# Two head loops written out: ACT and DVE without a loop, POOL with one

## What is computed

```
xn = layernorm(x)
x  = x + L0_attn(xn) + L0_ffn(xn)      # gated delta rule, 32 value heads on 16 key heads; MoE of 64 experts
xn = layernorm(x)
x  = x + L1_attn(xn) + L1_ffn(xn)      # 32 heads of 8, and 8 experts

L0_attn: mixed = conv4(silu)(xn @ w_qkv); q, k, v per head; l2norm(q), l2norm(k)
         for t: S = S*exp(g_t); d = (v_t - k_t S)*b_t; S = S + k_t d^T; o_t = q_t S
         out = (rmsnorm(o * silu(z)) * norm_w) @ w_out
```

## Time and profile before

| | us |
|---|---|
| median of three runs (lowest, highest) | 3089.01 (3083.01, 3095.82) |
| the profiled execution, its own time | 3097.86 |
| its span | 3096.1 |
| PE busy, of the span | 2761.4 (89%) |
| DVE busy | 2385.2 (77%) |
| ACT busy | 1765.9 (57%) |
| POOL busy | 1236.7 (40%) |
| mean granted TensorE clock | 0.963 of 2.4 GHz |

### The profile page before, as it was taken

One profiled execution on the slowest core, in us unless ns is written; L12 is line 12 of the kernel. 1 busy time (PEld: TensorE's weight loads), 2 busy tenths in 40 slices (PEclk: granted clock), 3 DMA queues, 4 the chain that ended last, 5 costly groups with the idle time before them and its releaser, 6 DMA issues. The chain is left out here.

```text
span 3096.1 us, 129193 instructions
## 1 busy us (share of the span) xinstructions
PE 2761.4 (89%) x52495; PEld 2287.1 (74%) x52496; DVE 2385.2 (77%) x5142; ACT 1765.9 (57%) x5625; POOL 1236.7 (40%) x1120
## 2 busy tenths in 40 slices
PE   2599989898999999999999999999999999967888
PEld 1477777777787878787878787878788888744555
DVE  7577787777877777777887878777778787638996
ACT  1366666666666666666666666666666666521111
POOL 4555555655333333333333333333333333335620
PEclk8799999999999999999999999999999999988999
DMA  4211111101111111111110111111111111163311
GB/s 170 73 52 55 42 41 31 31 27 29 44 30 42 30 44 30 44 30 44 30 44 30 44 30 37 29 37 34 39 34 41 34 41 34 34 228 98 115 63 41
DMA packets 94202, 155.58 MB, mean 50 GB/s; under 512 B 17238, under 2 KB 61829, under 8 KB 92403
## 3 DMA queue, kind: packets, MB, share of 16 engines
q1 hardware_dynamic: 69779, 112.45, 12.2%
q0 software_dynamic: 12288, 24.19, 2.5%
q10 hardware_dynamic: 11520, 10.49, 1.0%
HBM read 115.18 MB, written 41.29 MB: 51 GB/s over the span
## 5 line engine op out<-in xcount | busy, mean ns | idle before, releaser
L1278 DVE SCALAR_TENSOR_TENSOR p_y<-p_xr,p_cw,p_y 128x512 f32<-128x512 f32 x768 | 673.4, 885 | 44.3 <-ACT p_y L1027 23.8
L1085 ACT ACTIVATE p_Xs<-p_psI 128x256 f32<-128x256 f32 (+1 forms) x386 | 160.3, 415 | 523.0 <-PE p_psI L762 451.0
L714 PE MATMUL p_psF<-xnS,p_w_hl 128*128 128x512 f32 x1536 | 433.4, 419 | 21.1 <-PEq L586 21.1
L1504 POOL TENSOR_TENSOR p_E<-p_E,p_sj 128x512 f32<-128x512 f32 x128 | 131.8, 1050 | 744.2 <-DVE p_sj L1305 744.2
L714 PEld LDWEIGHTS p_psF<-xnS,p_w_hl 128*128 128x128 f32 x1536 | 278.0, 195 | 74.6 <-issue 21.7
L1323 DVE TENSOR_TENSOR p_ATP<-p_psF,p_E 128x512 f32<-128x512 f32 x256 | 166.5, 687 | 180.6 <-PE p_psF L749 171.6
L1512 POOL TENSOR_TENSOR p_M<-p_ATc,p_masks 128x512 f32<-128x512 f32 x128 | 170.4, 1336 | 308.4 <-ACT p_ATc L1065 308.4
L771 PE MATMUL p_psI<-p_Xs,p_DTc 32*32 32x32 f32 x16384 | 213.6, 196 | 66.6 <-issue 64.6
L762 PEld LDWEIGHTS p_psI<-p_Dc,p_M 32*32 32x32 f32 x16384 | 174.4, 107 | 130.9 <-issue 122.8
L771 PEld LDWEIGHTS p_psI<-p_Xs,p_DTc 32*32 32x32 f32 x16384 | 177.0, 107 | 121.0 <-issue 106.1
L762 PE MATMUL p_psI<-p_Dc,p_M 32*32 32x32 f32 x16384 | 205.5, 195 | 60.0 <-DVE p_DTc L1341 35.2
(11 more groups left out here) (328 smaller groups left out, 6541.1 us busy)
## 6 DMA issues: line engine op xcount, KB each, us to landing
p_ab<-decays SPq DMA_DIRECT2D x64, 512.0 KB, 5.3
p_w_raw<-in_w_in SPq DMA_DIRECT2D x17, 768.0 KB
expert_out<-p_ye ACTq DMA_DIRECT2D x80, 128.0 KB, 2.2
p_wgu<-in_w_gu SPq DMA_DIRECT2D x56, 176.0 KB
expert_in<-p_zero SPq DMA_DIRECT2D x16, 512.0 KB, 9.7
p_xe<-expert_in SPq DMA_DIRECT2D x56, 128.0 KB
p_wd<-in_w_down SPq DMA_DIRECT2D x56, 88.0 KB
p_wout<-in_w_out SPq DMA_DIRECT2D x16, 256.0 KB
```

The lines of the kernel that those rows point to most:

```text
L714: m = pe.matmul(b4(psF[f % 2][:, :]), w_hl[:, wp, kt, ty * P:(ty + 1) * P], xnS[:, xp, kt, :].rearrange("p (b t) -> p b t", b=B)[:, :, c * ...
L1085: act.activation(dst, src, ACT.Copy).then_inc(s["xs" if l < 5 else "join_xs"], 1)
L1278: m = dve.scalar_tensor_tensor(y[:, ty, :, :], xr[:, ty, :, tap:tap + P], cw[:, ty, tap:tap + 1], y[:, ty, :, :], ALU.mult, ALU.add)
```

## The change

ACT's and DVE's loops over the heads become Python loops like PE's. The calls of `announce` and the branch go, and every wait's value becomes a constant. `count[0]` is set to 0 for each head, as the emitted step did it once before. POOL keeps `heads_loop`. Below the first edit line numbers of ACT fall by 2 only after its loop, those of DVE's functions by 2, those of POOL and of layer 1 by 3.

```
-            with heads_loop(nc, "heads_act", mybir.EngineType.Activation, HK) as (kh, announce):
+            for kh in range(HK):
                 for c in range(NC):
-                    if c == NC - 1:
-                        announce()
                     step(kh, c)
...
-            with heads_loop(nc, "heads_dve", mybir.EngineType.DVE, HK) as (kh, announce):
+            for kh in range(HK):
+                count[0] = 0
                 for c in range(NC):
-                    if c == NC - 1:
-                        announce()
                     step(kh, c)
                 assert count[0] == DSTEPS, count[0]
```

## The result

The changed kernel takes 3072.3 us (median of 8 runs, 3066.4 to 3075.9) against 3088.3 for the kernel before (8 runs, 3083.0 to 3099.4): ratio 0.994, 95% interval 0.9926 to 0.9954, so 14 to 23 us faster, 16.0 by the medians. The prediction had 3075. The profiled execution took 3070.1 us, 2.2 under its median, where the one before was 9.6 over its own; so traces that differ by 27.8 us of span stand for 16.0 us, and only what repeats from head to head is read from them. Of the 27.8 us, 13.1 are PE's busy time with the same instructions, at a mean granted clock of 0.963 before and 0.969 after, and 14.7 are PE's idle time. The 16.0 us owe little to the clock: the changed kernel's eight runs have a mean of 0.968, and 23 runs of the kernel before, beside the first experiments, 0.967.

The account below looks back on a forecast made before the run. PE, busy for 89% of the span, bounds the kernel. Late register operations (9.2 us) and the passage between heads (4.4) sum to 13.6 us, taken from the median 3089.0 to predict 3075 us, range 3050 to 3092.

Parts of the forecast that it names:

- Register operations behind a late wait: Where an engine idles for a late semaphore, each register operation delays the data operation 0.08 us; together 9.2 us.
- Covered ones: Register operations beside running data operations, such as the 1712 at DVE's L1269, are worth 0.
- L1341: PE's 64 waits for DVE's transposes in the levels: half counted, 32 x 0.08 = 2.6 us.
- L1323: PE's 16 waits for DVE: two register operations behind PE's first product, 16 x 0.16 = 2.6 us.
- L1333: PE's 16 waits: ACT's copy in front has two register operations behind DVE's products, 16 x 0.16 = 2.6 us.
- keys from ACT: PE's 18 waits for keys: one register operation each, at ACT's evacuation or the silu, 18 x 0.08 = 1.4 us.
- The passage: Between heads: 0.17 us from DVE's earlier taps and 0.12 from ACT's kq, 0.29 x 15 = 4.4 us.
- The table load does not bound the passage: Between heads: DVE's taps bound, so ACT's 1.28 us load adds nothing; PE's wait moves from L897 to L739.
- The range of the forecast: Whole kernel: by the bounds of the prices, the forecast's own range is 3064 to 3084 us.
- rival A: Passage between heads: PE keeps the whole 1.1 us in each head, 16.5 us; time 3059; chance 0.28.
- B: PE's 79 stops before L771 set the pace; the gain shrinks to 0 to 5 us, 3087; chance 0.16.
- C: ACT's and DVE's written-out heads: fetching straight code stalls PE's path, 37 us less 13.6, time 3112; chance 0.11.

Follow-up runs that it names:

- run 10: Changed kernel with one register operation put back before the subtraction of each inverse level (255 places); ratio 0.9966 to the kernel before.
- run 6: Changed kernel with one covered register operation put back into the wait of every link of DVE's chains; ratio 0.992 to the kernel before.
- run 2: Kernel before with only DVE's heads written out, ACT keeping its loop and table loads; ratio 0.9967 to the kernel before, 10.2 us faster.
- run 7: Changed kernel with five register operations in a row before the subtraction of each inverse level; ratio 1.0175 to the kernel before.
- Run 1: Kernel before with only ACT's heads written out, DVE keeping its loop; ratio 0.9985 to the kernel before, 4.6 us faster.
- run 9: Changed kernel with 12 small copies before the Silu opening each head's ACT work, a delay without a load; ratio 0.9961 to the kernel before.
- half changes: Kernel before with only ACT's heads written out (ratio 0.9985), and with only DVE's written out (0.9967).
- runs 1 to 3: Kernel before with ACT's heads alone written out (0.9985), DVE's alone (0.9967); changed kernel with POOL's loop written out too (0.9942); ratios to the kernel before.
- run 8: Changed kernel with POOL's third L537 operation waiting for the next head's key taps, in POOL's loop only; ratio 0.9896 to the kernel before.
- runs 9 to 12: Changed kernel with 12 copies (0.9961); one late register operation a level (0.9966); POOL's third operation later, its loop written out (0.993); later, loop kept (0.9915).

## Why the prediction was right

The time was right to 3 us and the mechanism largely. That the sum came so near is in part luck: two terms were too large by 5.0 us together, and two too small by about 7. Its terms:

- **Register operations behind a late wait, 0.08 us each: right.** 0.087 us between 0.133 and 0.046 behind PE, in over 100 places; put back alone in run 10, the 0.13 returns. **Covered ones 0: right**, run 6.
- **L1341, 2.6 us: too small.** PE's wait fell by 4.1 (4.8 with DVE alone), and run 2 leaves some 7 us for it beside its passages. The step that failed is the count, 32 places: in run 7 half of the delay of all levels in which DVE waits for PE shows in PE's waits, and of such levels the kernel before has 124, so 62 x 0.087 = 5.4 us (an estimate).
- **L1323, 2.6 us: wrong, 0.** PE's wait before L739 for the products stayed at 5.0. In the kernel before and in the changed one, the product that PE waits for starts right behind PE's matmuls:

```profile
209.81 1.13 PE L749 MATMUL p_psF<-p_kq 128*128 128x256 f32 x4
210.97 1.29 DVE L1323 TENSOR_TENSOR p_ATP<-p_psF,p_E 128x512 f32<-128x512 f32 x2 [0.76 <-PE p_psF L749]
```

```profile
208.13 1.13 PE L749 MATMUL p_psF<-p_kq 128*128 128x256 f32 x4
209.30 1.29 DVE L1321 TENSOR_TENSOR p_ATP<-p_psF,p_E 128x512 f32<-128x512 f32 x2 [0.84 <-PE p_psF L749]
```

  0.03 and 0.04 us: this product, the step's second half, never had a register operation behind its late wait. The first half had (0.13 to 0.21 us behind PE before, 0.04 now, in most steps), and PE doesn't wait for that one. The prediction counted from the program's text, where the timeline would have told.
- **L1333, 2.6 us: wrong, 0.2** (5.2 to 5.0).
- **keys from ACT, 1.4 us: about right.** PE stands before L739 also in every step c = 1: 13.0 us in the trace before, 11.8 after.
- **The passage, 4.4 us: too small, 7.4.** The arms were right: no wait before L897, one of 0.85 before L739, which grew by 6.0 us (5 to 12 foretold); the first tap at 0.75; a later one at 1.64 (1.8 foretold). Two sizes were off. POOL holds a tap for 0.9 us and not 1.06, and with the tap's start at 2.97 that makes 0.34 us where 0.17 was expected. ACT's two register operations before kq made 0.155, not 0.12 (kq starts 0.19 behind the third tap before, 0.03 after).
- **"The table load does not bound the passage": true of the kernel before, not of the change.** Run 1 shows it free with DVE in its loop. In run 2, with DVE written out, ACT's loop costs 0.29 us of each passage (7.29 against 7.00), and it is the arm with the load that ends last there (L781 at 7.36; kq, with its register operations, is done at 7.00). A delay of 1.11 us in that place without a load or a loop costs 0.18 (run 9). The prediction counted both edits at once and so got the right sign; a load priced at 0 and left in would cost some 3 to 4 us (15 x 0.18 to 0.29, an estimate).

- **The range of the forecast, 3064 to 3084:** its lower end is no sum of the prices. By their dear ends, 13.8 and 16.5 us, it would be 3059, which stands under rival A.

Terms: 7.4 for the passage and 1.2 for the keys, from the traces, and about 7 for the levels, what run 2 leaves, make 15.6 of 16.0. The last is a remainder and known to 4 us only, so that the sum closes this well is chance.

Of the rivals, **A** (PE keeps the 1.1 us) is refuted by the wait for kq. **B** (the stops before L771 set the pace) would have had them above 75 us: they are 60.0, and 65.8 and 59.5 in the half changes. **C** (fetch of straight code) needed ACT or DVE idle with "issue" for 0.5 us and more off the passages, and a slower kernel; none of runs 1 to 3, in which up to three more engines are written out, is slower than its counterpart, and the queue moves fewer packets. One row has the sign that the prediction named: "ACT L1024 <- issue", 10.6 us in 10 pieces, nine of them over 0.5 us, not there before. Its longest, in the timeline of the changed kernel:

```profile
958.38 4.40 PE L714 MATMUL p_psF<-xnS,p_w_hl 128*128 128x512 f32 x12
...
961.39 0.60 ACT L1024 ACTIVATE p_xr<-p_psF 128x512 f32<-128x512 f32 x1 [2.96 <-issue]
```

PE was in the projection whose first half ACT evacuates there. In all ten pieces ACT starts 0.09 us behind the end of the sixth of its 12 matmuls; where the rows name PE, it starts 0.04 us behind the end of that same sixth matmul in 94 of 98. So these waits are for PE, and the sign was too loose; why they lost the name isn't shown.

The Trainium skill, "Runtime: NRT & Kernel Launch" (Instruction fetch mechanics), puts a stall behind a taken branch out of the fetched window. The 0.41 us of the earlier trace rows are gone, as that rule has it, but how much of them was such a stall isn't shown: the loop's own register operation, branch and first instruction on DVE take 40, 68 and 51 ns in the kernel before (L42, L43, L41, medians). Nor were they what the passage lost: POOL's turn hid a part of them, and PE got 0.20 from them as long as the load stood.

## What to carry to other kernels

Count a wait's overhead where the engine is idle when the awaited event comes, and find those places in the timeline, by the distance from the producer's end to the consumer's start; the same instruction is free everywhere else. At a join of two arms price each arm with the other shortened: half a change can show a third of the gain, and a covered cost is covered only by as much as its room (0.86 us here). After a change ask once more what is in the way: here it was an operation of POOL that could wait 2.2 us in the later heads, though not in the first. And run the kernel that you compare with on the same chip as each experiment: without that, effects of 3 to 8 us stay open here.

## What the runs showed of the hardware that was not expected

- DVE's taps and POOL's `tensor_tensor` take turns whichever comes first: the tap in progress ends in 0.75 us, the next one takes 1.64, and POOL 1.71 in place of 1.27. Moved off the keys' taps, POOL's operation meets the queries' taps the same way (POOL 1.72 at 1554.68 in run 8, and the second tap of the queries, at 1555.30, 1.65).
- A fused register operation isn't cheap by being one: 93 ns each at DVE's L1274 in run 7, 40 ns for a plain one there. How many operations of the program are in one isn't shown.
- The kernel that keeps PE waiting longest is also granted less clock: 0.954 to 0.960 in run 7 against 0.967 to 0.971 in run 6 on the same chip, where PE takes 42 us more for the same instructions.
- A load between Exp and Silu costs its 1283 ns and nothing around it.
- Another chip ran the same kernel 2.8% slower (3178 against 3090 us) at a mean granted clock of 0.949 to 0.957 against 0.964 to 0.969, and the variants run there have more of PE's stops that wait for nothing (80.1 to 85.1 us in 111 to 116 pieces before L771, in place of 60.0 in 79). The loss isn't spread evenly: in runs 9 to 12 the eleven later heads take 1741 to 1750 us, as on the first chips, while the three heads in front of them take 530 to 542 us in place of 483 (changed kernel) and 488 (kernel before). All variants run there were faster than the kernel before. Why that chip is slow in those heads was not tried.
